# Loading the tiles of the first four conv heads in parts

## The reference, cut to what matters

```python
qkv = jnp.moveaxis(jnp.concatenate([q, k, v], axis=-1), -1, 1)        # 1x1 projections of x
dw = lax.conv_general_dilated(qkv, dw_kernel, (1, 1), 'SAME', feature_group_count=3 * INNER, ...)
pw = lax.conv_general_dilated(dw, pw_kernel, (1, 1), 'VALID', feature_group_count=3 * NUM_HEADS, ...)
f = jnp.concatenate([qkv, pw], axis=1).reshape(B, -1, 3 * d, N)
...
scores = jnp.einsum('bhdn,bhen->bhde', value_pad, key_)
out = jnp.einsum('bhde,bhen->bhdn', scores, query)
out = out[:, :, :-1] / (out[:, :, -1:] + EPS)
```

## Time and profile before

| | |
|---|---|
| median of 3 runs | 4757.51 us (4748.52 to 4766.44) |
| the profiled execution's own time | 4761.0 us |
| its span, first to last instruction | 4759.2 us |
| TensorE matmuls busy | 4475.4 us, 94% |
| VectorE / ScalarE / GpSimd busy | 59% / 46% / 26% |
| mean granted TensorE clock | 0.971 |
| DMA | 1045.54 MB, 220 GB/s in the mean |

### The profile page before, as it was taken

The page is one execution under the profiler, slowest core; times in us unless marked ns, Lnnn a source line. Parts: engine busy times, 40 slices in busy tenths (PEclk is TensorE's granted clock), DMA queues, the critical chain, the costliest instruction groups (busy, mean ns, idle before and its releaser), DMA issues. The chain is left out here.

```text
span 4759.2 us, 70417 instructions
## 1 busy us (share of the span) xinstructions
PE 4475.4 (94%) x24296; PEld 3665.0 (77%) x24296; DVE 2811.9 (59%) x4023; ACT 2208.0 (46%) x3983; POOL 1239.6 (26%) x1030
## 2 busy tenths in 40 slices
PE   8999999999999999999999999589999999999968
PEld 7988988888888889888888888466666676666626
DVE  3354454454444444543544444279889978978996
ACT  3343333343333433433333334046576666666666
POOL 2442433433424424324334244000030020003003
PEclk9999999999999999999999999799999999999989
DMA  6685676676766766856767667767557746746613
GB/s 192 223 286 198 232 270 211 230 256 223 255 221 236 272 201 231 286 200 225 259 223 254 226 229 246 259 221 243 174 181 224 244 142 221 247 161 201 201 56 126
DMA packets 486662, 1045.54 MB, mean 220 GB/s; under 512 B 40624, under 2 KB 94512, under 8 KB 484016
## 3 DMA queue, kind: packets, MB, share of 16 engines
q1 hardware_dynamic: 486320, 1040.99, 65.1%
HBM read 665.02 MB, written 375.82 MB: 219 GB/s over the span
## 5 line engine op out<-in xcount | busy, mean ns | idle before, releaser
L807 POOL TENSOR_TENSOR toeplitz<-taps 128x512 f32<-128x512 f32 x768 | 895.7, 1193 | 932.3 <-PE bank L483 864.2
L483 PEld LDWEIGHTS bank<-toeplitz,columns 128*128 128x128 f32 x8192 | 964.3, 193 | 15.3
L483 PE MATMUL bank<-toeplitz,columns 128*128 128x128 f32 x8192 | 963.7, 276 | 0.0
L391 PE MATMUL bank<-x_hi,w_hi 128*128 128x512 f32 x1536 | 612.0, 398 | 19.8 <-DVE x_lo L655 19.8
L393 PE MATMUL bank<-x_lo,w_hi 128*128 128x512 f32 x1536 | 601.0, 391 | 0.0
L392 PE MATMUL bank<-x_hi,w_lo 128*128 128x512 f32 x1536 | 599.1, 390 | 0.0
L1530 POOL TENSOR_TENSOR centred<-centred,x_out 128x512 f32<-128x512 f32 x128 | 174.3, 1384 | 1606.8 <-ACT centred L1313 1605.1
L742 DVE TENSOR_SCALAR ckey_t<-bank 128x256 f32<-128x256 f32 x256 | 108.5, 424 | 807.5 <-PE bank L483 807.5
L473 PE MATMUL bank<-loaded,toeplitz 128*128 128x256 f32 x2048 | 510.9, 394 | 57.7 <-DMA loaded<-tiles_dram 42.1
L1163 PE MATMUL bank<-edge,w_branch 128*128 128x512 f32 x1024 | 483.2, 621 | 78.6 <-ACT edge L1261 78.6
L1149 PE MATMUL bank<-att_hi,w_proj_hi 128*128 128x512 f32 x1024 | 437.5, 427 | 62.3 <-DMA att_lo<-att_dram 51.2
(11 more groups left out here) (142 smaller groups left out, 7036.7 us busy)
## 6 DMA issues: line engine op xcount, KB each, us to landing
x_sb<-in_x_tiled SPq DMA_DIRECT2D x128, 1024.0 KB, 6.3
loaded<-tiles_dram SPq DMA_DIRECT2D x256, 433.5 KB, 5.9
tiles_dram<-tiles SPq DMA_DIRECT2D x112, 867.0 KB, 7.6
inverse<-inverse_dram SPq DMA_DIRECT2D x256, 256.0 KB, 7.7
att_dram<-out_hi SPq DMA_DIRECT2D x256, 256.0 KB, 4.1
att_dram<-out_lo SPq DMA_DIRECT2D x256, 256.0 KB, 5.1
att_hi<-att_dram SPq DMA_DIRECT2D x64, 1024.0 KB, 7.6
att_lo<-att_dram SPq DMA_DIRECT2D x64, 1024.0 KB, 10.5
```

The lines of the kernel that those rows point to most:

```text
L391: nc.tensor.matmul(banks[t][:, :], wh, xh, start=(k == 0), stop=False)
L483: last = nc.tensor.matmul(bank[:, v * M:(v + 1) * M], columns[:, h % 2, t - T_K, v + b, a * HT:(a + TO) * HT], w[:, t, d, :], start=(d == ...
L807: last = nc.gpsimd.tensor_tensor(toeplitz[:, h % 2, t, :].rearrange("p (d o r) -> p d o r", o=HD, r=PL), tap, point, ALU.mult)
```

## The change

SP now loads heads 0 to 3 in parts. `load_early` stands between the last chunk's K/V write and its Q write: it waits for the writes of the chunks before and loads rows 0 to 13 of each head (`EARLY`, 112 partitions). Behind the Q write, rows 14 and 15 of each head (`FINAL`) are loaded one by one, 8 partitions each. For this, `loaded` is laid out rows first (partition = row x 8 + channel) instead of channels first, in all loads; the taps are transposed to match on the host. The last `spill` of the stage moves behind these loads. The wait before them is for the last chunk's buffer alone. A head's semaphore in the first four counts three DMAs instead of one.

```diff
+        EARLY, FINAL = slice(0, PL - PL // NCH), slice(PL - PL // NCH, PL)
...
                     for part in parts:
+                        if part == (T_Q,):
+                            load_early(it)
                         for t in part:
                             sp.wait_ge(evac[t], NCH * it + j + 1)
...
-                def load_head(h):
-
-                    sp.dma_start(loaded[:, h % LR, :, :].rearrange("p t s -> p (t s)"),
-                                 dram["tiles"][h * HD:(h + 1) * HD].rearrange("i r n -> (i r) n")
+                def load_head(h, of):
+
+                    sp.dma_start(loaded[of.start * HD:of.stop * HD, h % LR, :, :].rearrange("p t s -> p (t s)"),
+                                 dram["tiles"][h * HD:(h + 1) * HD, of, :].rearrange("i r n -> r i n")
                                  ).then_inc(tiles_loaded[h % LR], 16)
+
+                def load_early(it):
+                    for n in range(TB):
+                        writes = 1 if n == buffer(NCH - 1) else tile_writes(n)
+                        sp.wait_ge(tile_written[n], 16 * START + 16 * tile_writes(n) * it + 16 * writes)
+                    for h in range(LR):
+                        load_head(h, EARLY)
...
-                        if conv_of is not None and j >= LATE:
+                        if conv_of is not None and LATE <= j < NCH - 1:
                             spill(conv_of, 1, j - LATE)
...
-                    for n in range(TB):
-                        sp.wait_ge(tile_written[n], 16 * START + 16 * tile_writes(n) * (it + 1))
+                    n = buffer(NCH - 1)
+                    sp.wait_ge(tile_written[n], 16 * START + 16 * tile_writes(n) * (it + 1))
 
                     for h in range(LR):
-                        load_head(h)
+                        for r in range(FINAL.start, FINAL.stop):
+                            load_head(h, slice(r, r + 1))
+                    if conv_of is not None:
+                        spill(conv_of, 1, NCH - 1 - LATE)
...
-                            load_head(h + LR)
+                            load_head(h + LR, slice(0, PL))
...
-                    pe.wait_ge(tiles_loaded[h % LR], 16 * (SH // LR) * it + 16 * (h // LR) + 16)
+                    pe.wait_ge(tiles_loaded[h % LR], 16 * (SH // LR + 2) * it + 16 * (h // LR) + 48)
...
-                    act.wait_ge(tiles_loaded[h % LR], 16 * (SH // LR) * it + 16 * (h // LR) + 16)
+                    act.wait_ge(tiles_loaded[h % LR], 16 * (SH // LR + 2) * it + 16 * (h // LR) + 48)
...
+    tap = tap.transpose(1, 2, 0, 3, 4)
```

## The result

The changed kernel takes 4821.48 us in the median of six runs (4818.14 to 4831.76), the kernel before 4758.83 (4748.52 to 4766.93). The ratio is 1.0134, with a 95% interval of 1.0117 to 1.0151: slower by 1.3%, where 4731 was forecast, and outside the range. The profiled execution has a span of 4818.6 us, 59.4 more than before. All of it is lost in the attention, whose last score matmul (L504 before) ends at 2988.9 us before and at 3048.1 now.

A forecast was written before the change was run, and what follows sets the result against it. Bound by TensorE, busy 94% of the span; only its idle or lower-clock stretches could give time back. Less idle at boundaries, 17.4 us, plus clock, 8.6, made 26 us off 4757.5: 4731 us, range 4704 to 4762.

The forecast's parts named there:

- At 380 GB/s, 4.1 us, from T-2.4 to T+1.7.: At each boundary, counted from the Q write's issue T: the four early loads, 1.55 MB, finish in the queue's gap.
- the slow end: At each boundary: early loads at 250 GB/s would end at T+3.8 and the Q write land at T+5.4.
- The early loads hold up the Q write: Rival, at the boundaries: one queue served in order; at 220 GB/s Q write lands T+6.3, +26 us, 4783; chance 0.08.
- Full loads by rows first: same packets in another order, landing four heads ahead. Nothing.: In the conv stages: whole loads in rows-first order cost 0 us.
- Head 0 has landed at T+5.6: At boundary 2 of the kernel before: when head 0's tiles are there, as ScalarE's `columns` starts.
- the tiles themselves come no sooner: At the boundaries: head 0 whole at T+5.75 against T+5.6 at best, early loads paying for the late Q write.
- the long kind: After boundaries: longer half-clock stretch, eight of them before, all with 3.8 us or more idle; expected to become short.
- The rival by which a branch costs the same whatever the loads do: At the loop's back edge on TensorE: 5.1 us branches not due to loads, time 4756; chance 0.15.
- The finer reading: At thirteen loop boundaries: TensorE's branch takes 5.1 us if the first load precedes it, 3.7 to 3.9 otherwise.
- The idle time of 37.1 us: TensorE's idle before L473 at sixteen boundaries: 37.1 against 54.5 us, a gain of 17.4.
- the clock's 8.6: Behind the boundaries: eight long half-clock stretches become short at 2.45 us idle, 8 x 1.07 = 8.6 us gained.
- The spill moved behind: nothing: Behind each boundary's loads: two issues of 256 KB may delay SP 1 to 2 us, covered, so 0 us.

The follow-up runs named there:

- e14: Kernel before with tiles in DRAM as head x row x channel, rows first, each whole load issued as two, 14 and 2 rows, none early: 4814.3 us, 1.0105.
- e1: Kernel before with every head still loaded whole but rows first, taps to match; no early loads, spill unmoved: 4788.8 us, 1.0072.
- e7: Changed kernel with tiles in DRAM as head x row x channel, four heads in parts as contiguous blocks, last two rows one load: 4789.5 us, 1.0061.
- e3: Changed kernel with head 0 alone in parts, heads 1 to 3 whole and rows first behind the Q write: 4763.7 us, 1.0006.
- e5: Kernel before with head 0 alone rows first and in parts, heads 1 to 15 as before, spill behind the loads: 4729.3 us, 0.9937.
- e9: As e7, but only heads 0 and 1 in parts; heads 2 and 3 whole behind the Q write: 4729.4 us, 0.9934.
- e12: As e5, but heads 0 and 1 instead of head 0 alone rows first and in parts: 4733.6 us, 0.9939.
- e11: As e7, but the four early loads issued right behind the Q write instead of in front of it: 4823.2 us, 1.014.
- e8: Kernel before with only the last spill moved behind the four loads: 4754.4 us, 0.9983.
- e10: As e7, but head 0 alone in parts, one early load and one of its last two rows: 4755.9 us, 0.999.
- e6: Kernel before with whole loads rows first, tiles in DRAM as head x row x channel, each load one contiguous block: 4745.7 us, 0.9971.

## Why the prediction was wrong

**What failed.** Two terms.

*"At 380 GB/s, 4.1 us, from T-2.4 to T+1.7."* The loads start at T-2.3 as said, and end at T+4.5 to T+5.7, mostly T+5.3: 7.5 us. The Q write then lands at T+6.7 and not T+3.3. The 380 came from a row of writes. The row for such loads was in hand: the stretch of before with its four whole loads moved 282 GB/s, and from 467.5 to 474.5, until they are through, it moves 261:

```profile
DMA packets 579, 1.83 MB, mean 261 GB/s; under 512 B 63, under 2 KB 63, under 8 KB 575
```

I named 250 as the slow end and took the fast one "since nothing else moves then". At 261 the 1.55 MB and the Q write's 0.3 end at T+4.8. No run prices the rest by itself; that packets of loads of 112 partitions take longer than whole ones' (0.20 us against 0.16 in e14) would give it. Head 0 is whole at T+8.9 in the middle of the thirteen loop boundaries, where the prediction had T+5.75. The rival *The early loads hold up the Q write* was right as a mechanism. It had the Q write at T+6.3 and the idle time up by some 18 us; measured are 6.7 and 21.2. I gave it 0.08.

*"Full loads by rows first: same packets in another order, landing four heads ahead. Nothing."* By e1 it costs 0.7%, about half of the loss; e7 against the changed kernel says the same (1.0061 and 1.0134). "Four heads ahead" was true of the loads themselves. But the queue is full for 35 us of each conv stage, and the taps behind them were just in time. No rival had it.

Two readings were off without deciding it. "Head 0 has landed at T+5.6" is boundary 2's: over the thirteen loop boundaries of before it lands at T+5.6 to T+8.5, T+7.5 in the middle. So "the tiles themselves come no sooner" was wrong too where the Q write isn't held up: in e3 head 0 is whole at T+4.7. And at boundary 15 L435 ends at T+4.46 and not T+4.2, 0.3 us of the sum.

**What followed from the first.** The branch is long in eleven of thirteen, with the early loads still in the queue when it begins; the clock falls in the long kind twelve times.

**What held.** The time from the first row load's issue to head 0 whole (T+3.3 to T+5.75 forecast, 2.2 us measured). That branches are short with nothing large ahead of them and can be long behind it: e3, e5, e9, e12 all 3.3 to 4.1, e11 7.0. The rival by which a branch costs the same whatever the loads do is out. The finer reading, that it depends on whether the branch or the first load comes first, is not enough: in e1 ten branches behind a load are short, and in e8 most lie between the two kinds. The Trainium skill's rule ("Runtime: NRT & Kernel Launch", Instruction fetch mechanics) that the fetch itself is forced stands too: no taken branch there took under 3.29 us. The idle time of 37.1 us comes once only one or two heads are loaded early (e3, e5, e9: 35 to 37), and the clock's 8.6 and more in e5. "The spill moved behind: nothing" held to 0.2% (e8), but as a sum: shorter branches against longer waits for GpSimd.

## What to carry to other kernels

Take a transfer's rate from a row of the same kind, loads from loads, and of the same shape; and before putting one ahead of something that is waited for, add its whole time on that queue. Before changing the form of a transfer that lands early, look whether the queue is full where it runs: there it costs its extra time to whatever is queued behind. Move ahead only what the first consumer needs: one or two heads of four gave the whole gain (e5, e9, e12), all four took it away and more. Even so measure each version: e10, with one head, got almost none of it.

## What the runs showed that was not expected

A 433.5 KB load to 128 partitions from one contiguous block moves its 3468 B packets in 0.16 us each in the mean around a boundary in before and e6 (0.21 in e10); the same bytes from a source of three levels, or as two DMAs of 112 and 16 or of 64 and 64 partitions, in 0.20 to 0.23. In a full queue that is 387 against 353 to 372 GB/s in the 13 us ahead of head 10, and 372 to 375 against 339 to 349 over all stages. Issue takes 0.43 to 0.44 us in the contiguous whole form, 0.54 with three levels, 0.63 where only 8 engines share the load, 0.59 for 64 partitions. A loop's back edge on TensorE costs 3.3 to 4.1 us with nothing large ahead of it (e3, e5, e9, e12), 3.5 to 4.4 with whole loads issued 0.4 to 0.6 us behind its begin (e6), and 7.0 in the middle with four loads of 379 KB just ahead (e11).
